# A gated-attention and expert kernel: the norm's scale steps are spread among VectorE's larger operations, and the value products are split around the second gate product

## What is computed

```python
def _layernorm(x, axis=-1, eps=1e-05):
    m = jnp.mean(x, axis=axis, keepdims=True)
    v = jnp.var(x, axis=axis, keepdims=True)
    return (x - m) / jnp.sqrt(v + eps)

# gated attention, x already normed and cut into groups of 32 tokens
v = silu(xc @ Wv + bv)
gate = silu(xc @ Wg + bg)
x_ = silu(xc @ Win + bin_)
quad_q, quad_k = x_ * g_qq + b_qq, x_ * g_qk + b_qk
lin_q, lin_k = x_ * g_lq + b_lq, x_ * g_lk + b_lk
attn = square(relu(where(causal_mask, 0, quad_q @ quad_k.T / 16)))
kv = cumsum(lin_k.T @ v, axis=groups) - itself
o = (attn @ v + lin_q @ kv) * gate
x = x + o @ Wout + bout
```

## Time and profile before

| | |
|---|---|
| median of 3 runs | 1536.02 us (1535.35 to 1537.2) |
| the profiled execution | 1544.41 us |
| its span, first to last instruction | 1542.6 us |
| PE busy | 1456.9 us, 94% |
| VectorE busy | 1068.5 us, 69% |
| ScalarE busy | 918.2 us, 60% |
| GpSimd busy | 282.6 us, 18% |
| mean granted TensorE clock | 0.983 |

### The profile page before, as it was taken

The page is one execution under the profiler, slowest core; times in us unless marked ns, Lnnn a source line. Parts: engine busy times, 40 slices in busy tenths (PEclk is TensorE's granted clock), DMA queues, the critical chain, the costliest instruction groups (busy, mean ns, idle before and its releaser), DMA issues.

```text
span 1542.6 us, 43235 instructions
## 1 busy us (share of the span) xinstructions
PE 1456.9 (94%) x18426; PEld 1010.9 (66%) x18426; DVE 1068.5 (69%) x2176; ACT 918.2 (60%) x1723; POOL 282.6 (18%) x325
## 2 busy tenths in 40 slices
PE   6999889999999999999999999999999999999956
PEld 5889774465677755657777556577775565775746
DVE  7875047787766678876666788766667887777632
ACT  4665566555666656556666566566665656666512
POOL 4156523413000031030000311300003013000170
PEclk9999999999999999999999999999999999999987
DMA  7501221111000010010000101100001011000011
GB/s 219 185 18 47 71 62 35 43 28 44 16 16 16 16 52 23 21 45 16 15 16 16 53 23 34 45 16 15 16 16 53 22 36 43 15 19 12 2 38 35
DMA packets 44302, 58.29 MB, mean 38 GB/s; under 512 B 8199, under 2 KB 32624, under 8 KB 43984
## 3 DMA queue, kind: packets, MB, share of 16 engines
q1 hardware_dynamic: 34960, 38.27, 8.9%
q0 software_dynamic: 9152, 17.26, 4.0%
HBM read 22.14 MB, written 19.32 MB: 27 GB/s over the span
## 4 chain that ended last, share of the span: by engine, by line
PE 81%; DVE 9%; ACT 5%; another core or an unknown queue 3%; issue 2%; DMA 0%; DVEq 0%; ACTq 0%; SPq 0%
PE bank L1075 28%; PE bank L1088 24%; PE bank L1003 5%; DVE nmx L1110 4%; PE bank L1008 3%; PE bank L1017 3%; PE bank L401 3%; PE bank L373 2%; ACT prob L1119 2%; PE bank L1230 2%; PE bank L1226 2%; PE bank L1187 1%; ACT hT L495 1%; PE bank L774 1%
## 5 line engine op out<-in xcount | busy, mean ns | idle before, releaser
L1119 ACT ACTIVATE prob<-bank,nmx 128x1024 f32<-128x1024 f32 x512 | 570.2, 1114 | 440.7 <-DVE nmx L1110 439.4
L1110 DVE TENSOR_REDUCE nmx<-bank 128x1 f32<-128x1024 f32 x512 | 625.8, 1223 | 211.0 <-PE bank L1075 195.8
L1088 PE MATMUL bank<-prob,vsc 64*64 64x512 f32 x4096 | 643.4, 590 | 4.7 <-DVE ctxT L1137 3.0
L1075 PE MATMUL bank<-q,k 64*64 64x512 f32 x2048 | 531.7, 593 | 14.5 <-ACT prob L1119 13.2
L1075 PE MATMUL bank<-q,ks 64*64 64x512 f32 x2048 | 529.1, 592 | 0.0
L1088 PEld LDWEIGHTS bank<-prob,vsc 64*64 64x64 f32 x4096 | 233.7, 133 | 130.2 <-issue 63.5
L1003 PE MATMUL bank<-xT,wqkv_sb 64*64 64x256 f32 (+1 forms) x1560 | 211.7, 434 | 0.0
L1075 PEld LDWEIGHTS bank<-q,ks 64*64 64x64 f32 x2048 | 135.7, 132 | 85.1 <-issue 24.2
L1647 POOL DMA_INDIRECT yg<-yslots,row_ring x64 | 65.1, 1017 | 587.1 <-PE bank L1075 571.7
L1075 PEld LDWEIGHTS bank<-q,k 64*64 64x64 f32 x2048 | 133.2, 133 | 53.9 <-ACT prob L1119 27.6
L1003 PEld LDWEIGHTS bank<-xT,wqkv_sb 64*64 64x64 f32 x1560 | 91.8, 133 | 87.7 <-issue 32.2
(11 more groups left out here) (264 smaller groups left out, 1646.1 us busy)
## 6 DMA issues: line engine op xcount, KB each, us to landing
ks<-k SPq DMA_DIRECT2D x64, 256.0 KB
yslots<-slots_sb SPq DMA_DIRECT2D x7, 640.0 KB, 3.6
slots_sb<-xslots SPq DMA_DIRECT2D x5, 640.0 KB, 4.5
xslots<-xhat_r POOLq DMA_DIRECT2D x5, 512.0 KB, 7.1
yslots<-xhat_r POOLq DMA_DIRECT2D x5, 512.0 KB, 12.2
w_sb<-in_w SPq DMA_DIRECT2D x1, 2048.0 KB, 9.4
wqkv_sb<-in_wqkv SPq DMA_DIRECT2D x1, 2048.0 KB, 18.8
xslots<-xhat_r,row_s POOLq DMA_INDIRECT x112
```

Source lines behind the costliest of these rows:

```text
L1075: ins = nc.tensor.matmul(bank[rows(c), SC[h][n], :], kk[r, cols(2 * j + c, HD)], qst[pi % 2][r, cols(n, HALF)], start=True, stop=True)
L1088: ins = nc.tensor.matmul(bank[rows(h), CX[n], :], vsc[s][rows(r), rows(h)], prob[g % 3][h][rows(r), cols(n, HALF)], start=(j == 0 and firs ...
L1110: nc.vector.tensor_reduce(nmx[:, 2 * s + h:2 * s + h + 1], bank[:, SC[h][0]:SC[h][0] + 2, :], mybir.AxisListType.XY, ALU.max, negate=True) ...
L1119: nc.scalar.activation(prob[g % 3][h][:].rearrange("p (n c) -> p n c", c=HALF), bank[:, SC[h][0]:SC[h][0] + 2, :], ACT.Exp, bias=nmx[:, 2 ...
```

## The change

`newton_vector` and `shift_vector` are cut into 13 numbered pieces (`rstd_piece`, `RSTD_PIECES` = 12 and the shift as piece 12; piece 1 holds two instructions, so there are still 14). Each piece waits for the step counter as before. In rows 1 to 3 the pieces stand: 0 behind the statistics, 1 to 3 behind each of the three features, 4 to 7 behind each of the four values, 8 and 9 behind the quadratic masks, 10 and 11 behind the sums, 12 (the shift) behind the first state. In row 0: 0 behind the statistics, 1 and 2 behind the quadratic masks, 3 and 4 behind the sums, 5 to 11 behind the seven states, 12 behind the last of them.

On TensorE the order becomes: projection, gate of e = 1, positions, values of tiles 0 to 3, the wait for `f_kept`, gate of e = 0, values of tiles 4 to 7. The transposes of `lkT` now wait for all four gate halves (`a_gs` at 4r + 4) instead of two. ScalarE reads the gates in the new order.

```diff
-        def route_rstd_vector(v, step, k):
+        def route_rstd_piece(v, step, k, i):
             c0, n = (min(N_ROUTE, N_MAIN[k + 2]), 2 * T) if k + 2 < B else (N_ROUTE, T)
-            if k > 0:
+            if i == 0 and k > 0:
                 v.wait_ge(lf_xhat, 2 * k)
                 v.wait_ge(la_xhat, 2 * (k + 2))
-            newton_vector(v, step, c0, NEWTON, True, n)
-            shift_vector(v, step, c0, lf_rstd, n)
+            if i == RSTD_PIECES:
+                shift_vector(v, step, c0, lf_rstd, n)
+            else:
+                rstd_piece(v, step, c0, n, i)
...
-            pe.wait_ge(a_gs, 4 * r + 2)
+            gate(1)
+            if places is not None:
+                positions(pe, places + 1, POS_A)
+            values(0)
+            if places is not None:
+                pe.wait_ge(f_kept, places + 1)
+            gate(0)
+            values(1)
+            pe.wait_ge(a_gs, 4 * r + 4)
             pe.wait_ge(a_feat, 3 * r + 1)
...
-            for e in range(EH):
+            for n, e in enumerate((1, 0)):
                 for h in range(2):
-                    a.wait_ge(a_gproj, 4 * r + 2 * e + h + 1)
+                    a.wait_ge(a_gproj, 4 * r + 2 * n + h + 1)
...
+            beside(0)
             v.wait_ge(a_xs, 2 * r + 2)
-            for dst, c in ((lkT, 9), (qkT, 5), (qqT, 3)):
+            for i, (dst, c) in enumerate(((lkT, 9), (qkT, 5), (qqT, 3))):
                 nc.vector.tensor_scalar(dst[:], base[:], ca[:, c:c + 1], ca[:, c + 1:c + 2], ALU.mult, ALU.add).then_inc(a_feat, 1)
+                beside(1 + i)
             for k in range(4):
...
-            if route is not None:
-                route_rstd_vector(v, step, route)
+                beside(4 + k)
...
+            second(0)
...
+                beside(8 + h)
+                second(1 + h)
...
+                beside(10 + h)
+                second(3 + h)
...
+                if t == 1:
+                    beside(RSTD_PIECES)
+                second(4 + t)
+            second(RSTD_PIECES)
             for e in range(EH):
-                if e == 1 and row == 0:
-                    second_rstd_vector(v, step)
```

More of the change, by code:

```diff
@@ L722, in a_tensor, with gate @@
                 nc.tensor.matmul(o, wa_hi[:, 0:P], x_lo, start=False, stop=True).then_inc(a_xproj, 1)
-            if places is not None:
-                positions(pe, places + 1, POS_A)
-                pe.wait_ge(f_kept, places + 1)
-            for e in range(EH):
+            def gate(e):
                 c = slice(WG + e * P, WG + (e + 1) * P)
@@ L846, in a_vector, with beside, second @@
             r = row + 1
+            def beside(i):
+                if route is not None:
+                    route_rstd_piece(v, step, route, i)
+            def second(i):
+                if row == 0:
+                    second_rstd_piece(v, step, i)
             if row == 0:
```

47 lines of the change are left out of this document (34 added, 13 removed).

## The result

The changed kernel takes 1533.42 us (median of 20 runs, 1527.89 to 1537.23) where the kernel before, run beside it, takes 1536.83 us (median of 20, 1533.33 to 1539.10): a ratio of 0.9977, 95% interval 0.9970 to 0.9984, or -3.4 us. It is faster, but by under a third of the 11.4 us forecast, and 1533.42 lies above the range of 1520.5 to 1530.5. Yet the profiled execution took 1533.56 us, where the sum gave 1533.0 against the profiled execution of before. That agreement is luck: of the 10.8 us between these two executions 6.1 are there at the end of the stage that was changed, and the rest comes in work that the change doesn't touch.

The account below looks back on a forecast made before the run. Both VectorE and TensorE were taken as near-critical, so each must get faster. Rows 0 to 3 gave 3.95 + 0.35 + 3.7 + 3.4 = 11.4 us off the median 1536.02: 1524.6 us, range 1520.5 to 1530.5.

Parts of the forecast that it names:

- A dealt step at 0.08 us: VectorE's 14 short instructions: each costs 0.08 us between independent neighbours, bounds 0 and 0.20, against some 0.20 in one block.
- the rival at 0.20: VectorE, rows 0, 2 and 3: each dealt step costs 0.20 us wherever it stands; together -4.7 to -6.2 us, about 1530.5; chance 0.10.
- Row 0: Up to the output projection: it starts 2.4 us earlier and saves 1.55 us of slow clock; -3.95 us, bounds -2.0 and -4.2.
- second rival: GpSimd's bias addition delays the second `xT_lo`, or the clock falls, keeping part of row 0's gain; -6.5 to -9.8 us; chance 0.15.
- Row 1: The state chain starts 0.6 us earlier and stops pacing the products of e = 0; -0.35 us, bounds 0 and -0.5.
- Row 2: From residual to e = 0: 14.05 us instead of 17.31, bound by `lk`, -3.25; e = 0's products -0.45; together -3.7 us.
- Row 3: The same as in row 2: residual to e = 0 from 16.98 to 14.05 us, and -0.45 for e = 0; -3.4 us.
- The base of the sum: The 11.4 us taken off the median 1536.02; the profiled execution's extra 8.4 us put down to the execution, not this stage.
- After the stage nothing is lost: Behind the stage is TensorE's work, untouched; the gain should arrive at the end undiminished unless some wait there doesn't move.
- its getting smaller: End of row 3: moved work may lose VectorE's 5.86 us wait; another 1.5 to 3 us, about 1522; chance 0.12.
- its standing at a fixed time: End of row 3: if the wait's end at 137.22 isn't moved, everything won is waited away; 1536, no change; chance 0.06.
- The late shift: Rows 1 to 3: shift behind the first state, covered by 0.25 us; a rival had it slower, about 1540, chance 0.04.

Follow-up runs that it names:

- Each half of the change alone: Kernel before with only the dealt steps on VectorE: 1535.85 us, ratio 0.9994; with only the new order of TensorE and ScalarE: 1537.78 us, 1.0008; before 1536.37 us.
- five profiles of before's order: Two profiles of the kernel before and three of kernels with its order and a change on GpSimd alone; three of the five have the half clock in rows 0 and 2.
- nine profiles of the changed code: Profiles of kernels with the changed kernel's code up to row 1's `xT_lo`, one with 64 idle increments in front; in five it waits for GpSimd, 2.9 us.
- the three comparisons of the table: Changed kernel against before, by profile: first against first, third against second, second against second; spans -10.8, -3.4 and -6.1 us.
- the dealt steps alone: Changed kernel with TensorE and ScalarE in the order of the kernel before, only VectorE's steps dealt out: 1535.85 us, ratio 0.9994 to before.
- the first pair: First profiles of the kernel before and of the changed kernel: -10.2 us at the first gate of row 3, span 1542.6 to 1531.8 us.
- The held-bias kernel: Changed kernel with GpSimd's bias additions held until VectorE's first state of row 1: 1467.21 us, ratio 0.9955 to before; at the other level 1535.00 us, 0.9990.
- the padded start of one: Changed kernel with 128 increments of an unused semaphore ahead of TensorE's first wait, which delayed the start by some 10 us: 1475.61 us, ratio 1.0009 to before.

## Why the prediction was right or wrong

**What bounds the kernel: right.** Both engines had to get faster. Each half of the change alone gives -0.5 and +1.4 us, both -3.9, and 0.7, 1.3 and 5.2 us at the second sum of row 3.

**A dealt step at 0.08 us: right**, and the rival at 0.20 falls. Each dealt step moves its neighbour by 0.08 us, the chain of states hides its steps wholly (0.53 us from state to state), and VectorE is free for the values 6.92 us after the residual in row 2 (forecast 6.7). The rule of the Trainium skill that was weighed, "VectorE: DVE Perf Modes", section "The DRAIN you can't avoid", doesn't describe this trace as the prediction gave it; the section adds that a next operation which isn't held starts earlier, and the 0.08 us agree with that. What cost 0.20 us was the dependence of one short step on the step before, not their number.

**Row 0: right in the profile read, wrong as a fixed term.** Shift at 32.93 (33.15 forecast), no idle time before the projection (37.50; 37.6), projection 3.84 us, residual -3.9 us (-3.95). But both of its parts come in some executions only. The 1.55 us of clock are there in three of five profiles of before's order. And the second `xT_lo` is free of GpSimd in four of nine profiles of the changed code. The prediction had this as its second rival, with the right size ("half a microsecond late, and it ends at 44.0"; the residual then started at 43.70), and gave it 0.15; it is the commoner case. Where the clock rises early in row 0, before pays for its half clock and the changed kernel is free; where it rises late, neither is so, and row 0 gains 0.3 us instead of 3.9. The Trainium skill, "SBUF — State Buffer", section "Terms", agrees: the 2.3 to 2.9 us of an `xT_lo` go to 0.69 when GpSimd's addition is moved away.

**Row 1: right**, -0.4 (-0.35).

**Row 2: right in mechanism, 3.1 for 3.7 in the first profile, 1.0 against a profile of before without the half clock.** From the residual to e = 0 it takes 86.27 - 71.59 = 14.68 us, forecast 14.05. The missed step: the linear scores (L792) wait 0.78 us for VectorE's last read of the values, and the quadratic ones 0.24 for `qqT`, waits that the sum left out of TensorE's chain; `lk`, which the sum had as the bound, ends at 82.87, 0.4 us before the states' products start, and 0.2 us later than forecast. The products of e = 0 take 89.61 - 86.27 = 3.34 us (forecast 3.4). And the 17.31 us of before, from which 3.25 were taken off, held about 2.2 us of slow clock, which two of the five profiles of before's order haven't. This is the largest false term, and it could have been seen: the prediction used the clock against the change ("if TensorE's clock falls as it does now"), but never asked whether before pays for it in every execution.

**Row 3: 2.8 for 3.4**, by the same missed wait (0.87 us here).

**The base of the sum: wrong.** "8.4 us longer than the median, which I put down to the execution and not to this stage." Of the 7.8 us between the two profiles of before, 2.8 lie ahead of the second sum of row 3 and 3.5 ahead of the last residual. The sum took the 11.4 us off a median in which such executions are a part, and not all.

**After the stage nothing is lost: wrong, for the stop.** The prediction said that "what is won here should arrive at the end undiminished, unless some wait there doesn't move", and the sum took the gates of row 3 to the last residual as unmoved. That stretch grew by 4.1, 4.8 and 0.4 us in the three comparisons of the table. The stop was in the trace of before; the prediction saw it, and gave 0.12 to its getting smaller and 0.06 to its standing at a fixed time, which would have waited away everything. Truly it is in between: not at a fixed time (the gate of e = 1 was at 137.22, then 127.72), but of another size: from the first gate to the last 7.9 and 6.6 us before, 8.6, 7.0, 8.6 and 8.7 after, and 4.9 to 5.0 where there is none. Much of the price is the clock behind it. In three of the four profiles of the changed kernel TensorE stands at the half clock for 6.8 us behind the stop, and from the last gate to the last residual they take 9.8 to 9.9 us; the fourth, without it, takes 7.2, and profiles without a stop 6.8. What makes the stop longer isn't shown: it isn't simply an earlier row, since before's longer one came in the later row (first gate at 129.97, and 127.13).

**The late shift: covered, as forecast.** In row 2 it comes 14.3 us after the residual (forecast 14.0), and the transposes of `xhat_r` don't wait. It doesn't even with the dealt steps alone, where the shift of row 3 comes later still.

Put together, with means over few profiles, and so an estimate: 11.4 were forecast; 1.2 less, by the missed wait for the most part, is the 10.2 of the first pair. Over all profiles the first gate of row 3 starts at 128.8 us in the five of before's order and at 121.2 in the nine of the changed code, which is 7.6: the half clock and GpSimd, each in some executions, take 2.6. From that gate to the last residual it takes 14.0 us before (two profiles) and 17.5 after (five) where there is a stop, and 11.7 and 11.8 where there is none: the stop takes another 3.4. That leaves 4.2, and 3.4 to 3.9 us were measured in four comparisons; where nothing stops, 6.8 and 6.3.

So three steps failed, the largest last: TensorE's chain in rows 2 and 3 left out a wait (1.2 us); the slow clock of before and a free `xT_lo` were taken as there in every execution (2.6 us); and the wait at the end of row 3 was taken as unmoved, so that all that is won arrives (3.4 us).

**What stays open.** Scatters in an unbroken run go with the stop: it moved with them in one profile and wasn't there when they were paced in another, both at the first level. What they and TensorE's signals share isn't shown. It isn't the amount of data: in 117 to 127 us of the changed kernel the DMA engines are busy for 9%. Nor was it settled why the stop never shows at 1474 us, or why an early rise of the clock in row 0 goes with the half clock later. The plain changed kernel wasn't timed at that level. The held-bias kernel was the best there (0.9955), but not at the other level (0.9990), so no version is shown to beat the changed kernel everywhere.

## What to carry to other kernels

Short dependent steps on VectorE cost their latency when they stand together and 0.08 us each when independent work stands between them; dealing them out pays only where the engine that feeds this one gets faster in the same place. Before you add up savings, profile the kernel before several times, and the changed one too: a term that rests on a slow clock, or on two engines missing each other by half a microsecond, is there in some executions only, and the median holds a part of it. In each profile look first at when the clock rises. And a stall that the profile can't name is not a constant: take it away by an experiment (hold or pace whatever runs beside it) and measure the change without it.

## What the runs showed of the hardware

An unbroken run of GpSimd's indirect scatters, one each 1.28 us, goes with 4 to 6 us in which VectorE and ScalarE aren't released by TensorE products that are recorded as done, and TensorE itself then stands for 0.5 to 4 us, and once in each such profile for 10 to 16. It shows where the kernel before takes 1536 to 1540 us, and not where it takes 1474: there three profiles have the same run of scatters beside row 3 and a fourth has it beside the experts, without a stop, and none of the seven has idle time of TensorE at "issue", apart from the padded start of one.

The granted clock falls to 1.2 GHz for 3.4 us in some executions and not in others, after the same waits of TensorE: 1.84 and 0.82 us of idle time ahead of row 0's projection, 5.37 us for the projection in one profile and 3.74 in the other. Which it is goes with the time at which the clock first rose, 16.0 to 16.5 us in the three that fall, 17.3 and 18.1 us in the two that don't.

VectorE's `xT_lo` beside GpSimd's addition takes up to 2.9 us instead of 0.69, and whether they meet is decided by 0.7 us. The residual (which reads a PSUM bank) and the statistics aren't held: in the first profile of the changed kernel GpSimd's addition runs from 40.68 to 43.11, and beside it two residual halves take 1.29 us from 40.77 and eight statistics 1.65 us from 42.21, as elsewhere.
